# Row transposes and logits of the router moved by one slot, and one routed chunk of the last stage by three

## The reference

```python
def _L0_ffn_ref(hidden_states, gate_w, gate_bias, We_gate, We_up, We_down, Ws_gate, Ws_up, Ws_down):
    x = hidden_states.reshape(-1, h)
    tidx, tw = _gate(x, gate_w, gate_bias)       # sigmoid(x @ gate_w.T), top 4 groups, top 8 experts
    w_dense = zeros((T, E)).at[rows, tidx].add(tw)
    def body(acc, ws):
        wg, wu, wdn, cw = ws
        hmid = silu(x @ wg) * (x @ wu)
        return acc + cw[:, None] * (hmid @ wdn)
    y = scan(body, 0, (We_gate, We_up, We_down, w_dense.T))
    return y + silu(x @ Ws_gate) * (x @ Ws_up) @ Ws_down
x = x + 0.5 * _L0_ffn_ref(_layernorm(x), ...)
x = x + _L0_attn_ref(_layernorm(x), ...)         # 16 heads of 64, causal softmax
x = x + 0.5 * _L0_ffn_ref(_layernorm(x), ...)
```

## Time and profile before

| | |
|---|---|
| median of 3 runs | 1664.81 us (1664.76 to 1666.91) |
| the profiled execution | 1664.28 us, its span 1662.5 us, mean clock 0.983 |
| PE busy | 1575.8 us, 95% of the span |
| DVE, ACT, POOL busy | 1199.7, 777.1, 670.6 us |
| first stage | 0 to about 565 us (dense to 405 us, quads after it) |
| last stage | from 1143 us; its quads from 1242 to 1396 us |

### The profile page before, as it was taken

How to read it: one execution, slowest core, us unless ns; L and a number is a source line. 1 busy time by engine, 2 the same in 40 slices (tenths; PEclk the granted TensorE clock), 3 DMA queues, 4 the chain that set the end, 5 groups by cost and what they waited for, 6 DMA issues and landing times. The chain is left out here.

```text
span 1662.5 us, 27254 instructions
## 1 busy us (share of the span) xinstructions
PE 1575.8 (95%) x8683; PEld 1017.4 (61%) x8683; DVE 1199.7 (72%) x3446; ACT 777.1 (47%) x2105; POOL 670.6 (40%) x931
## 2 busy tenths in 40 slices
PE   5899999999999899999999998997998999999999
PEld 2444444444888677777777776774447896444443
DVE  4687888765455478899898978764776855778675
ACT  2333223222444477777777766774224443223222
POOL 1000088887000323443333205544881002888840
PEclk9999999999899899999999999999999999999999
DMA  9999555552566300010000001103464765656652
GB/s 184 198 254 231 146 130 141 137 142 76 152 189 189 97 17 25 25 28 22 21 22 24 14 1 33 38 31 96 117 153 132 194 188 138 145 139 147 150 132 64
DMA packets 202043, 181.31 MB, mean 109 GB/s; under 512 B 39408, under 2 KB 154288, under 8 KB 201904
## 3 DMA queue, kind: packets, MB, share of 16 engines
q1 hardware_dynamic: 175056, 132.34, 33.3%
q0 software_dynamic: 16384, 33.59, 7.3%
q10 hardware_dynamic: 10464, 13.63, 2.5%
HBM read 121.83 MB, written 57.67 MB: 108 GB/s over the span
## 5 line engine op out<-in xcount | busy, mean ns | idle before, releaser
L840 ACT ACTIVATE f_hid<-banks 128x512 f32<-128x512 f32 (+1 forms) x264 | 157.6, 597 | 502.0 <-PE banks L800 501.7
L481 POOL DMA_INDIRECT x_rows<-r_xk,r_idx x256 | 266.1, 1040 | 139.8 <-issue 53.6
L862 DVE TENSOR_TENSOR f_hid<-banks,f_hid 128x512 f32<-128x512 f32 (+1 forms) x264 | 181.5, 688 | 153.5 <-ACT f_hid L840 153.2
L796 PE MATMUL banks<-r_xT_d,gu 128*128 128x512 f32 x528 | 276.0, 605 | 3.9 <-DMA wd<-in_L_ffn_We_down 2.3
L812 PE MATMUL banks<-f_hid,wd 128*128 128x512 f32 x528 | 272.2, 599 | 5.7 <-DVE f_hid L875 5.6
L800 PE MATMUL banks<-r_xT_d,gu 128*128 128x512 f32 x528 | 273.9, 601 | 0.0
L517 POOL DMA_INDIRECT f_g<-y_rows,r_idx x128 | 129.8, 1014 | 161.8 <-DMA y_rows<-f2q_yq 132.3
L875 DVE TENSOR_TENSOR f_hid<-f_mix_wide,f_hid 128x512 f32<-128x512 f32 x256 | 175.6, 686 | 26.0 <-DMA f_mix_wide<-mix_rows 23.7
L517 POOL DMA_INDIRECT a_g<-y_rows,r_idx x128 | 125.2, 978 | 160.6 <-POOLq L1602 105.6
L812 PEld LDWEIGHTS banks<-f_hid,wd 128*128 128x128 f32 x528 | 99.6, 192 | 140.4 <-issue 123.1
L800 PEld LDWEIGHTS banks<-r_xT_d,gu 128*128 128x128 f32 x528 | 100.9, 191 | 130.1 <-issue 127.0
(11 more groups left out here) (237 smaller groups left out, 2842.4 us busy)
## 6 DMA issues: line engine op xcount, KB each, us to landing
f_mix_wide<-mix_rows SPq DMA_DIRECT2D x124, 512.0 KB, 6.7
x_rows<-zero ACTq DMA_DIRECT2D x12, 1024.0 KB, 6.2
f1q_xq<-x_rows SPq DMA_DIRECT2D x48, 256.0 KB, 3.1
y_rows<-f1q_yq SPq DMA_DIRECT2D x48, 256.0 KB, 2.4
f2q_xq<-x_rows SPq DMA_DIRECT2D x48, 256.0 KB, 3.1
y_rows<-f2q_yq SPq DMA_DIRECT2D x48, 256.0 KB, 2.4
x_rows<-r_xk,r_idx POOLq DMA_INDIRECT x256
wd<-in_L_ffn_We_down SPq DMA_DIRECT2D x7, 512.0 KB, 9.9
```

The costliest lines, as they stand in the source:

```text
L481: nc.gpsimd.indirect_dma_start(x_rows[:, :], bass.IndirectOffsetOnAxis(ap=b.idx[:, f, CT * k + t, j:j + 1], axis=0), b.xk[:, k, t, :], Non ...
L796: nc.tensor.matmul(gate_bank[g % 3][0:rows, :], w["gu"][:, 0, experts, :].rearrange("p e f -> p (e f)"), x, start=True, stop=True)
L840: nc.scalar.activation(d.hid[0:rows, g % HIDS, :], gate_bank[g % 3][0:rows, :], ACT.Silu)\
L862: nc.vector.tensor_tensor(d.hid[0:rows, g % HIDS, :], up_bank[g % 3][0:rows, :], d.hid[0:rows, g % HIDS, :], ALU.mult).then_inc(gated, 1)
```

## The change

Two numbers of the step table change: the turn goes from 2 to 3 slots behind the moments, the logits from 4 to 5. The routing steps, and all on DVE and POOL in the first stage, stay where they are. The start of chunk 5 in the last stage goes from slot 3 to slot 6, so its moments, normalisation, turn, logits, routing and turn of the weights go to slots 6, 7, 9, 11, 12 and 21. The places among the quads are written so that they stay at 10 and 12.

```diff
-T_MOMENTS, T_APPLY, T_TURN, T_LOGITS, T_ROUTE = 0, 1, 2, 4, 6
+T_MOMENTS, T_APPLY, T_TURN, T_LOGITS, T_ROUTE = 0, 1, 3, 5, 6
...
-SECOND_AT = {5: 3, 7: 2 * SLOTS + 1}
+SECOND_AT = {5: 6, 7: 2 * SLOTS + 1}
...
             for j in range(QUAD_STEPS):
                 quad(j)
-                if j == Q_AT + T_TURN + 2:
+                if j == Q_AT + T_TURN + 1:
                     turn_xn(among)
-                if j == Q_AT + T_LOGITS + 2:
+                if j == Q_AT + T_LOGITS + 1:
                     logits(among)
```

## The result

| | before | after |
|---|---|---|
| median of 5 runs, us | 1664.81 (1662.63 to 1668.29) | 1654.7 (1653.0 to 1658.58) |
| ratio | | 0.9937, 95% interval 0.9918 to 0.9956 |
| profiled execution, its span, us | 1664.28, 1662.5 | 1653.0, 1651.3 |

The account below looks back on a forecast made before the run. PE was taken to bound most of the span, POOL's scatter the last stage up to its load. First stage -11.3, chunk 5 0 and chunk 7 +1.5 sum to -9.8 us: median 1655.0 us, range 1652.5 to 1657.

Parts of the forecast that it names:

- What bounds it, and that time freed before the scatter is kept and time freed beside it is given back: Whole kernel: PE leads, POOL's scatter sets the pace at the last stage's load; first-stage gains stay, last-stage ones are worth 0.
- Chunk 1: 0.: First stage, turn from slot 5 to 6: 2.32 us wait removed, worth 0, since DVE's product waits for a transfer.
- Chunk 4: -4.3.: First stage, turn from slot 14 to 15: slot 16 starts 4.3 us sooner, 1.7 us of it clock; about 1.5 us waiting left.
- Chunks 5, 6, 7: -4.5: First stage: waits of 1.22, 1.22 and 2.08 us before the three turns all go, 4.5 us gained.
- P_o: -0.9: First stage: chunk 7's logits pass to slot 41, so the transposed P_o no longer waits behind them, 0.9 us gained.
- chunk 2: -1.6: First stage, turn from slot 49 to 50: 1.6 us gained; 0.8 us more wait at the count offset by the logits.
- Sum of the first stage, -11.3: First stage: gains of 4.3, 4.5, 0.9 and 1.6 us; scatters start that much sooner, the 4.35 us load wait stays.
- Last stage, chunk 5: 0.: Moments from slot 3 to 6: PE 9.7 us sooner, but waits 14.8 us at the load, so worth 0; POOL's cover 0.4 us.
- POOL waits: Last stage: POOL waits for slot 6's moments, costing 2.4 us, total 1657.4; chance 0.13.
- Scatter chain: 0.: Last stage: the 68 scatters keep their 104.9 us; bounds 5.8 us less to about 2 more.
- the rival: Last stage: scatter chain shortens as DVE idles at its end, up to 5.8 us, total 1649.2, likelier 1652; chance 0.07.
- Chunk 7: +1.5.: Last stage, turn from slot 69 to 70: PE waits 1.6 us for DVE behind the turn of y, costing 1.5 us.

Follow-up runs that it names:

- e5: The change, but chunk 1 of the first stage keeps its old turn and logits slots; 1804.95 us (one run) against 1814.11 before.
- e4: The kernel before, without the memsets between the last stage's scatters; 1652.26 us, ratio 0.9919.
- e2: The kernel before with only the last stage's new slots, the first stage keeping its old ones; 1666.87 us, ratio 1.0009.
- e11: The change, but chunk 4 of the first stage keeps its old turn and logits slots; no whole time given, first scatter 3.2 us later than the change.
- e9: The change, but the last stage's weighing of routed rows starts in slot 21, not 16; no whole time given, load 110.0 us after stage start (change 110.3).
- e10: The change, but chunk 5 of the last stage starts in slot 8, not 6; 1808.49 us, ratio 0.9969.
- e6: The change, but all of the last stage's chunk 7 starts one slot earlier; no whole time given, turn of y to end 173.3 us (change 171.0).
- e13: The change without memsets between scatters in both stages, weighing from slot 21, chunk 7's turn and logits one slot earlier; 1635.9 us, ratio 0.9816.
- e3: The change, without the memsets between the last stage's scatters; 1640.67 us, ratio 0.9854.
- e12: The change, but only the turn and logits of the last stage's chunk 7 are one slot earlier; 1655.15 us, one run.
- e14: The change without the memsets between the last stage's scatters, measured a second time; 1641.3 us, ratio 0.9839.
- e1: The change in the first stage only, the last stage keeping its old slots; 1654.06 us, ratio 0.9931.
- the second set: Four of the follow-up kernels, run beside the kernel before at 1814.11 us, with attention about 150 us longer, cause open.

## Why the prediction was right, and where its steps were off

- **What bounds it, and that time freed before the scatter is kept and time freed beside it is given back**: right, shown by the two stages apart (0.9931 and 1.0009) and by the shorter scatter, which brings 3.5 us of the second back.
- **Chunk 1: 0.** Right (e5). The mechanism was stronger than said: the landing of one load of mix rows paces the stage up to chunk 4's rows.
- **Chunk 4: -4.3.** Counted from the landing of that load, slot 16 comes 4.3 us sooner than before, as forecast, 4.0 against e4, and 2.5 against e2 and e11, where the clock did not fall behind the turn: the 1.7 us of clock in this term come in some executions and not in others. On the span's clock it was -3.0, since the load landed at 60.81 us in place of 59.56. What was wrong is the wait: I had 1.5 us before the turn, and there was none. The turn still started when DVE's rows were there (74.38 us; forecast 73.1, plus the later landing), but PE had spent its time before: it waited 3.34 us for the product, and its clock stood at 0.64 from 61.5 to 65.7 us. I had set this delay from chunk 1's move at "wait longer", without the clock behind it; it cost nothing, because PE would have waited for the rows.
- **Chunks 5, 6, 7: -4.5; P_o: -0.9; chunk 2: -1.6.** The starts of slots 16, 24, 32, 40 and 44 give -1.29, -1.28, -2.11 and -0.91, sum 5.6 against 5.4. Chunk 2 between slots 44 and 53 -1.8. Right, with the count's 0.77 us: from slot 16 to the first scatter 7.2 us are gone in every new first stage, forecast 7.0.
- **Sum of the first stage, -11.3**: counted from the landing to the first scatter, -11.4 against the profile before, -11.1 against e4 and -9.6 against e2. On the span's clock -10.2 at the scatter, by the later landing, which follows no kernel (59.6 to 61.8 us with the old first stage, 59.2 to 62.3 with the new); at the load -11.1, because its wait was 1.1 us shorter, which I had held constant. That these two cancel is luck.
- **Last stage, chunk 5: 0.** Right in time. The wait at the load, forecast at 14.8, was 9.65: I had named DVE's routing beside the weighing as something "that may stall PE some us", but not priced it. It is 2.80 us at the turn of the weights and, in some executions, the clock behind it (e9: 13.40). The cover of POOL's rstd, forecast at 0.4 us, is 0.1, and in three of the six other profiles with chunk 5 at slot 6 and the memsets it is missing by 0.27 to 0.54 us: the rival "POOL waits" happens, at a tenth to a quarter of its price of 2.4 us.
- **Scatter chain: 0.** 104.9 and 104.5 us; over the other runs with memsets and without the late moments of e10 103.6 to 106.7. That the long dispatches come from DVE's work, which the rival had, is right, and the traces show from which. The 14 profiles have 952 dispatches in this chain. Of the 349 that start while DVE is in a TENSOR_TENSOR whose inputs both lie in SBUF, 171 last over 1.1 us; of the 603 others one does (1.57 us, such an operation starts 0.05 us after it). The 253 that start while DVE is idle take 0.95 to 0.97 us. Timeline of POOL and of DVE in the changed kernel:

```profile
1191.50 1.43 POOL L481 DMA_INDIRECT x_rows<-r_xk,r_idx  x1 [0.17 <-issue]
...
1194.88 0.96 POOL L481 DMA_INDIRECT x_rows<-r_xk,r_idx  x1 [0.17 <-issue]
```

```profile
1191.40 0.69 DVE L875 TENSOR_TENSOR f_hid<-f_mix_wide,f_hid 128x512 f32<-128x512 f32 x1
...
1194.52 0.68 DVE L862 TENSOR_TENSOR f_hid<-banks,f_hid 128x512 f32<-128x512 f32 x1
```

The first dispatch starts inside a product with both inputs in SBUF and takes 0.47 us more; the second starts inside one that reads PSUM and takes none. The change moves DVE's work, but the two meet as often: 14 dispatches over 1.1 us before and 13 after, 5.1 and 4.9 us more in sum. So the chain keeps its length, and its spread comes in part from how these meetings fall (7.2 us more in e6, 4.1 in e11). By the Trainium skill ("SBUF — State Buffer", Who interferes with whom) a DVE operation in a two-port mode that was issued first blocks GpSimd until it ends, and one with two inputs in SBUF contends with a GpSimd instruction that reads SBUF. The traces agree for the second kind: in most of these dispatches the lengthening is what is left of the operation at the start, less 0.12 us (0.59 us left, 0.47 longer). The page also says that a tensor_tensor did not stall a DMA when it was probed; here it does. That DVE idles while PE waits at the load shortened nothing: with 13.40 us of wait (e9) the chain took 104.2 us, 12 dispatches over 1.1 us.
- **Chunk 7: +1.5.** Right, 1.54 us of wait and 1.6 between slots; the clock stayed at 1.00.
- **Not forecast:** -2.8 in the first stage's quads and +1.4 in attention. Next section.

The total was closer than its parts, in part by luck: -9.8 forecast, -10.1 by the medians, -11.2 by the two profiled spans.

## What to carry to other kernels

A step moved away from a wait is worth its wait only if what comes last downstream is paced by the engine that waited: find the next wait of that engine, and what releases it, before counting. Where a queue of fixed length (here 68 dispatches at 1.46 us) ends a part, shorten the queue first; only then do the waits beside it have a price. And when two users of one scratch buffer meet in a slot, move the one that has slack, but alone: moving its whole chain put DVE's steps elsewhere and lost more than the wait. To compare two traces, count from the last event that both wait for (here the landing of one load), not from the start: the landing alone moved by 3 us between executions.

## What the runs showed of the hardware

- **A wait costs twice, and the second part varies between executions.** The loaded quads of the first stage are the same work in all kernels. Granted clock in their first 23 us, and their length up to attention: 1.00 and 143.2 us (no wait, e13); 0.93 and 144.2 to 144.8 (after, e3, e11, e12, e14, waits 3.3 to 3.7 us); 0.85 and 145.8 to 146.2 (e1, e6, e9, 3.1 to 3.7 us); 0.81 to 0.83 and 146.4 to 147.6 (before, e2, e4, e5, e10, 3.3 to 4.4 us). So the -2.8 us of the change's profile are its 0.93 against 0.82, but e5 and e10, with the new first stage, have 0.82 and 0.81: it isn't a sure gain. The last stage's loaded quads do the same: 141.0 us at 1.00 (no wait; e3, e4, e14), 142.5 to 143.0 at 0.91 to 0.93, 144.7 to 145.2 at 0.80 to 0.83. In rows, the changed kernel and before, first 23 us of those quads, PEclk the third figure from the end:

```profile
405.85:428.85 23.00, 23.00 (x169) 20.64 (x170) 10.06 (x21) 10.26 (x23) 0.00 (x0) 0.93 0.46 132
```

```profile
416.97:439.97 23.00, 23.00 (x152) 20.67 (x153) 9.05 (x20) 9.38 (x21) 0.00 (x0) 0.82 0.40 116
```

- **Attention varies by itself**: 577.3 to 580.5 us over the ten profiles outside the second set, 578.9 before and 580.3 after; +1.4 is inside that.
- **The 99 slots start at either clock.** After the same 0.83 us of idle time the first slot's gate products took 1.10 us in the change and 2.04 us in e12, whose first 10 us stood at 0.83. It costs 1.6 us in some executions of the same code (this last part takes 267.0 to 267.1 us in the change, e3 and e10, and 268.6 to 268.7 in e2, e5, e9, e11 and e14).
- **A memset of 328 ns between two dispatches cost 0.2 us of pitch each, not 0.33 us**: without it the idle time between dispatches rose from 0.17 to 0.30 us, and the median pitch went from 1.46 to 1.26 us.
- **A DVE operation with both inputs in SBUF holds up a scatter dispatch that starts inside it**: 171 of 349 such dispatches last over 1.1 us (to 1.50), one of 603 others. A product of the same size that reads PSUM, a reduction or an idle DVE leave them at 0.97 us at most. The four short operations of line 268 (one input, rows 128 long) cost the one dispatch that starts inside them 0.13 us, in all fourteen profiles.
